# Four tables of places by kind of slot, the next head's norm at the end of short slots, and the experts' rows transposed two parts ahead

## The reference

```python
x = x + xcond(layernorm(x), cond, ctx)        # 6 layers
x = x + ffn(layernorm(x), ...)                # 8 experts, top 2 of 8, capacity 640

def xcond(x, emb, context):
    for i in range(6):
        xn = adaln(x, emb, n1_w[i], n1_b[i])
        q, k, v = split(xn @ qkv_w[i].T)                      # 16 heads of 16
        x = x + attn(rope(q), rope(k), v) @ so_w[i].T
        xn = adaln(x, emb, n2_w[i], n2_b[i])
        q, k, v = rope(xn @ cq_w[i].T), rope(context @ ck_w[i].T), context @ cv_w[i].T
        x = x + attn(q, k, v) @ co_w[i].T
        xn = adaln(x, emb, n3_w[i], n3_b[i])
        x = x + gelu(xn @ f1_w[i].T + f1_b[i]) @ f2_w[i].T + f2_b[i]

def adaln(x, emb, w, b):
    g, be = split(emb @ w.T + b)
    return ln(x) * (1 + g) + be

def ffn(x):      # router, then per expert: gelu(rows @ w1 + b1) @ w2 + b2, gated and added to the tokens' rows
```

## Time and profile before

| | |
|---|---|
| median of 3 runs | 4456.39 us |
| lowest, highest | 4449.91, 4459.43 us |
| profiled execution | 4442.28 us, span 4440.6 us |
| busy TensorE, VectorE, ScalarE, GpSimd | 89%, 65%, 58%, 19% |
| mean granted TensorE clock | 0.962 |
| layers, to the end of slot 48 | about 4070 us from the start |
| experts' rows begin to be loaded | 4242.3 us |

### The profile page before, as it was taken

How to read it: one execution, slowest core, us unless ns; L and a number is a source line. 1 busy time by engine, 2 the same in 40 slices (tenths; PEclk the granted TensorE clock), 3 DMA queues, 4 the chain that set the end, 5 groups by cost and what they waited for, 6 DMA issues and landing times. The chain is left out here.

```text
span 4440.6 us, 68492 instructions
## 1 busy us (share of the span) xinstructions
PE 3940.5 (89%) x20630; PEld 1833.7 (41%) x20630; DVE 2907.1 (65%) x4711; ACT 2561.9 (58%) x4302; POOL 857.7 (19%) x518
## 2 busy tenths in 40 slices
PE   3699999999999999999999999999999999997467
PEld 1233344533344533345433345433345433354355
DVE  3777766677766678766678766678766677752311
ACT  1376656667666567666567665567666566654122
POOL 4312121112121112211111211111211121200133
PEclk7799999999999999999999999999999999999689
DMA  5354323244323244332244332244332344410234
GB/s 162 85 135 108 97 69 78 63 108 120 87 78 72 60 113 119 87 80 65 67 108 116 94 72 66 68 108 116 97 75 59 74 129 111 109 30 13 83 99 95
DMA packets 271578, 396.39 MB, mean 89 GB/s; under 512 B 28312, under 2 KB 218400, under 8 KB 270880
## 3 DMA queue, kind: packets, MB, share of 16 engines
q1 hardware_dynamic: 263904, 382.18, 34.1%
q0 software_dynamic: 7296, 9.51, 1.3%
HBM read 226.63 MB, written 170.67 MB: 89 GB/s over the span
## 5 line engine op out<-in xcount | busy, mean ns | idle before, releaser
L837 ACT ACTIVATE prob<-ps 128x512 f32<-128x512 f32 x3072 | 1768.2, 596 | 1225.2 <-PE ps L761 1207.6
L999 DVE TENSOR_REDUCE negmax<-ps 128x2 f32<-128x1024 f32 x1536 | 1836.7, 1219 | 217.6 <-PE ps L788 195.2
L761 PE MATMUL ps<-qstack,kstack 114*128 114x512 bf16 x3072 | 1162.4, 389 | 100.1 <-ACT prob L837 84.8
L774 PE MATMUL psv<-prob,v 128*32 128x512 f32 x6144 | 829.5, 612 | 0.0
L761 PEld LDWEIGHTS ps<-qstack,kstack 114*128 114x128 bf16 x3072 | 284.6, 97 | 1190.3 <-ACT prob L837 794.5
L616 POOL TENSOR_TENSOR rot<-ropep 128x512 f32<-128x512 f32 x96 | 122.5, 1276 | 2486.7 <-DVE ropep L1032 2467.7
L788 PE MATMUL ps<-kstack,qstack 49*128 49x512 bf16 x3072 | 496.8, 388 | 97.9 <-DVE negmax L999 76.8
L736 PE MATMUL side<-anat,wf 128*128 128x256 f32 x1536 | 377.1, 388 | 9.9 <-DVE hT L1037 8.9
L1037 DVE TENSOR_SCALAR hT<-side,f1b 128x256 f32<-128x256 f32 x384 | 168.2, 479 | 303.6 <-PE side L736 303.6
L747 PE MATMUL side<-wf,hT 128*128 128x256 f32 x1536 | 347.9, 379 | 2.8 <-DVE x L1044 1.6
L736 PEld LDWEIGHTS side<-anat,wf 128*128 128x128 f32 x1536 | 285.6, 192 | 65.7 <-DVE hT L1037 30.9
(11 more groups left out here) (158 smaller groups left out, 3722.1 us busy)
## 6 DMA issues: line engine op xcount, KB each, us to landing
bounce<-parts SPq DMA_DIRECT2D x480, 256.0 KB, 2.5
qstack<-bounce SPq DMA_DIRECT2D x384, 192.0 KB, 5.5
kstack<-bounce SPq DMA_DIRECT2D x384, 192.0 KB, 6.1
bounce<-low SPq DMA_DIRECT2D x96, 256.0 KB, 2.1
ctxT<-in_ctxT SPq DMA_DIRECT2D x24, 512.0 KB, 3.9
nw<-in_nwT SPq DMA_DIRECT2D x18, 512.0 KB, 11.3
w<-in_w SPq DMA_DIRECT2D x16, 512.0 KB, 4.8
wself<-in_wself SPq DMA_DIRECT2D x24, 256.0 KB, 4.0
```

What stands on the lines that cost most here:

```text
L761: nc.tensor.matmul(ps2[:, n % RING2, :], kk[0:ROWS, h, kt * P:(kt + 1) * P], q[0:ROWS, h, :], start=True, stop=True).then_inc(s_p2full, 1)
L774: mm = nc.tensor.matmul(psv[32 * i:32 * i + 32, 0, :], v[j % 2][:, kt, (HD + 1) * h:(HD + 1) * h + 32], prob[:, 4 * (u % 2) + i, :], start ...
L837: nc.scalar.activation(prob[:, 4 * (u % 2) + i, :], ps2[:, n % RING2, :], ACT.Exp, scale=HD ** -0.5).then_inc(s_prob, 1)
L999: nc.vector.tensor_reduce(out_at, ps1[:, 2 * (n % 2):2 * (n % 2) + 2, :], AX, ALU.max, negate=True).then_inc(s_p1free, 1)
```

## The change

The two tables become four, by the kind of the slot and of the one before: `SHORT`, `SHORT_AFTER_LONG`, `LONG` and `LONG_AFTER_LONG`. Each also holds the places of the shift (M), the splits, gelu and the norms. In short slots the norm for the **next** slot's HT stands at halves 22 to 28 (`LN_NEXT`), unless the next slot follows a long one; a slot after a long one does its own at halves 0 to 5 (`LN_HT`). In long slots HT moves from 6 and 8 to 11 and 12, T2 and O move two halves earlier, LT and its norm move by one or two. In short slots HQ, HK, T2 move by up to two halves. VectorE does both reductions of a unit first when its even half has a chunk of HQ, HK, O, F1 or F2. In the experts `gather_T` and `read_T` of part n+2 stand ahead of `outputs` and `biased` of part n.

```diff
-SHORT_PLACES = {
-    "HV": [1, 3], "T1": [2, 4, 5, 7], "HT": [6, 8], "HQ": [9, 10], "HK": [12, 14],
-    "T2": [15, 17], "O": [19, 21],
+SHORT = {
+    "M": [23, 0], "HV": [1, 3], "T1": [2, 4, 6, 8], "HT": [5, 7], "HQ": [9, 11], "HK": [13, 15],
+    "T2": [16, 18], "O": [19, 21], "SPLIT": (13, 15, 19, 21),
+    "LN_NEXT": dict(stats=[22, 22, 23, 23], aggregate=24, guess=25, newton=26, tiles=[27, 27, 28, 28]),
 }
-LONG_PLACES = {
-    "HV": [1, 3], "T1": [2, 4, 5, 7], "HT": [6, 8], "T2": [9, 10], "O": [11, 12], "HQ": [13, 14],
-    "HK": [15, 16], "LT": [17, 18], "F1": [19, 20, 21, 22, 23, 24, 25, 26], "F2": [27, 28, 30, 31],
+SHORT_AFTER_LONG = {
+    "M": [24, 0], "HV": [1, 3], "T1": [2, 4, 6, 8], "HT": [7, 9], "HQ": [10, 12], "HK": [14, 16],
+    "T2": [17, 18], "O": [20, 21], "SPLIT": (14, 16, 20, 22),
+    "LN_HT": dict(stats=[0, 0, 0, 0], aggregate=1, guess=2, newton=3, tiles=[3, 4, 4, 5]),
+    "LN_NEXT": dict(stats=[22, 22, 23, 23], aggregate=24, guess=25, newton=26, tiles=[27, 27, 28, 28]),
 }
-SHORT_SHIFT, LONG_SHIFT = (23, 0), (29, 0)
-NORM_PLACES = {
-    "HT": dict(stats=[0, 0, 1, 1], aggregate=1, newton=3, tiles=[3, 3, 4, 4]),
-    "LT": dict(stats=[12, 12, 12, 12], aggregate=13, newton=15, tiles=[15, 15, 16, 16]),
+LONG = {
+    "M": [29, 0], "HV": [1, 3], "T1": [2, 4, 5, 6], "T2": [7, 8], "O": [9, 10], "HT": [11, 12], "HQ": [13, 14],
+    "HK": [15, 17], "LT": [16, 18], "F1": [19, 20, 21, 22, 23, 24, 25, 26], "F2": [27, 28, 30, 31],
+    "SPLIT": (16, 18, 20, 22), "GELU": (23, 27),
+    "LN_LT": dict(stats=[10, 10, 10, 10], aggregate=11, guess=12, newton=13, tiles=[13, 14, 14, 15]),
 }
-GUESS_PLACES = {"HT": 2, "LT": 14}
-SHORT_SPLIT = (13, 15, 18, 20)
-LONG_SPLIT = (16, 18, 20, 22)
-GELU_PLACES = (23, 27)
+LONG_AFTER_LONG = {**LONG, "LN_HT": dict(stats=[0, 0, 0, 0], aggregate=1, guess=2, newton=3, tiles=[3, 4, 4, 5])}
...
+            after_long = k < 2 or is_ffn(k - 1) or k == 2
+            return ((SHORT, SHORT_AFTER_LONG), (LONG, LONG_AFTER_LONG))[is_ffn(k)][after_long]
...
-                    if p1:
+                    both = any(what in ("HQ", "HK", "O", "F1", "F2") for what, c in plan[2 * u])
+                    if p1 and half == 0:
                         maximum(k, at)
-                        if at == 17:
-                            shift_parts(k, 0)
+                        if both:
+                            maximum(k, at + 1)
+                    if p1 and half == 1 and not both:
+                        maximum(k, at)
+                    if p1 and at == 16:
+                        shift_parts(k, 0)
...
             gather_T(0)
             hidden(0)
+            gather_T(1)
             for n in range(len(PARTS)):
                 if n + 1 < len(PARTS):
-                    gather_T(n + 1)
                     hidden(n + 1)
+                if n + 2 < len(PARTS):
+                    gather_T(n + 2)
                 outputs(n)
...
+            read_T(0)
+            read_T(1)
             gates(0)
-            read_T(0)
             for n in range(len(PARTS)):
-                if n + 1 < len(PARTS):
-                    if n % 2 == 1:
-                        gates((n + 1) // 2)
-                    read_T(n + 1)
+                if n + 2 < len(PARTS):
+                    read_T(n + 2)
+                    if n % 2 == 0:
+                        gates(n // 2 + 1)
                 biased(n)
```

More of the change, by code:

```diff
@@ L394, in is_ffn, with places_of, norm_steps @@
             return k >= 2 and is_cross(k - 2)
+        def places_of(k):
+            after_long = k < 2 or is_ffn(k - 1) or k == 2
+            return ((SHORT, SHORT_AFTER_LONG), (LONG, LONG_AFTER_LONG))[is_ffn(k)][after_long]
+        def norm_steps(k):
+            steps, places = [], places_of(k)
+            if "LN_HT" in places and k + 1 < 2 * NJ:
+                steps.append((k, "HT", places["LN_HT"]))
+            if "LN_LT" in places:
+                steps.append((k, "LT", places["LN_LT"]))
+            if "LN_NEXT" in places and "LN_HT" not in places_of(k + 1) and k + 2 < 2 * NJ:
+                steps.append((k + 1, "HT", places["LN_NEXT"]))
+            return steps
         def slot_chunks(k):
@@ L399, in slot_chunks @@
             tail, head = k >= 2, k + 1 < 2 * NJ
-            places = LONG_PLACES if is_ffn(k) else SHORT_PLACES
+            places = places_of(k)
             plan = {i: [] for i in range(2 * SLOT_UNITS)}
@@ L416, in slot_chunks @@
                 put("HT", "HQ", "HK")
-            shift_places = LONG_SHIFT if is_ffn(k) else SHORT_SHIFT
             if p2:
-                plan[shift_places[1]].append(("M", 1))
+                plan[places["M"][1]].append(("M", 1))
             if p1:
-                plan[shift_places[0]].append(("M", 0))
+                plan[places["M"][0]].append(("M", 0))
             if is_ffn(k):
@@ L917, in slot @@
                 ffn = is_ffn(k)
-                splits = LONG_SPLIT if ffn else SHORT_SPLIT
+                places = places_of(k)
+                splits = places["SPLIT"]
                 for at in range(2 * SLOT_UNITS):
@@ L930, in slot @@
                         side_work(k, what, c)
[L931 to L934, removed]
+                    for of, what, steps in norm_steps(k):
+                        if at == steps["guess"]:
+                            rstd_guess(of, what)
                     if head and at in splits:
@@ L937, in slot @@
                         (hi, mid)[step](k + 1, n)
-                    if ffn and at in GELU_PLACES:
-                        gelu(k, GELU_PLACES.index(at))
+                    if ffn and at in places["GELU"]:
+                        gelu(k, places["GELU"].index(at))
             run_slots(act, place, head0, slot)
@@ L962, in stats @@
                         wait_read(dve, place, k, "O", 1)
+                    elif "LN_HT" not in places_of(k):
+                        wait_read(dve, place, k - 1, "O", 1)
                     elif steps[0]:
@@ L1068, in slot @@
                 plan = slot_chunks(k)
-                ffn = is_ffn(k)
                 for at in range(2 * SLOT_UNITS):
                     u, half = divmod(at, 2)
-                    if p1:
+                    both = any(what in ("HQ", "HK", "O", "F1", "F2") for what, c in plan[2 * u])
+                    if p1 and half == 0:
                         maximum(k, at)
-                        if at == 17:
-                            shift_parts(k, 0)
+                        if both:
[4 more added lines that the diff above has]
+                        shift_parts(k, 0)
                     for what, c in plan[at]:
                         side_work(k, what, c)
[L1078 to L1081, removed]
+                    for of, what, norm in norm_steps(k):
                         for t in range(TT):
-                            if at == places["stats"][t]:
-                                stats(k, what, t)
-                        if at == places["aggregate"]:
+                            if at == norm["stats"][t]:
+                                stats(of, what, t)
+                        if at == norm["aggregate"]:
                             aggregate(what)
-                        if at == places["newton"]:
-                            normalise(k, what)
+                        if at == norm["newton"]:
+                            normalise(of, what)
                         for t in range(TT):
-                            if at == places["tiles"][t]:
-                                normed(k, what, t)
+                            if at == norm["tiles"][t]:
+                                normed(of, what, t)
                 if p1:
```

## The result

The changed kernel takes 4464.73 us (median of 20 runs, 4457.06 to 4469.98), the kernel before, run beside it, 4454.17 us (20 runs, 4445.0 to 4467.27). The ratio is 1.0023, with a 95% interval of 1.0015 to 1.0031: slower by 0.2%. The forecast was 4384 us.

A forecast was written before the change was run, and what follows sets the result against it. TensorE, busy 89% of the span, was taken as the bound, so only its waits cost time. Terms -20 - 29 - 7 - 4 - 12 = -72 us gave 4370 us profiled, 4384 us as median, range 4325 to 4440.

The forecast's parts named there:

- Moved past queues: SyncE's writes and loads move with `mid`; cover before the next slot's scores shrinks; priced at nothing, else 6 x 1 us.
- The other two signs that I had named: Signs of being wrong: short slots above 66.4 us, or long slots moving by over 1 us.
- Experts: Experts: transposes of part n+2 ahead of `outputs` of part n remove the copy wait from parts 2 to 15; -20 us.
- Short slots, halves 4 to 21: Short slots: waits of 4.21 us go, new ones of 1.75 come; gain 2.45 us a slot.
- Halves 22 to 31: End of short slots: the next head's norm on VectorE and its guess on ScalarE cost 0.85 us a slot.
- the six after long slots: Short slots after long ones keep a norm at the start and gain less: 1.2 us each, -7 us.
- Long slots: Long slots: `normed` leaves GpSimd's residual but new waits come; 0.2 us a slot, -4 us, plus -12 from fewer clock dips.
- The sum: Whole kernel: all terms together -72 us on the profiled execution, 4442.3 to 4370; as median 4384 us.
- (e): Rival: the clock falls more often, every long slot taking 99.0 us; 4427 us, chance 0.09.
- (d): Rival: VectorE becomes the bound at its new places, the norm ending short slots showing fully; +56, 4512 us, chance 0.08.
- (a): Rival: the new waits in the layers do not come; 4336 us, chance 0.16.
- The port rule: VectorE and GpSimd share ports; the first to start blocks the other; third tile of long slots held up to 1.26 us.

The follow-up runs named there:

- the run that mends it alone: Changed kernel with the load of M's rows ahead of the next head's ten loads in SyncE's queue, in short slots: 4407.78 us, ratio 0.9899.
- the run at half 19: Changed kernel with the first shift of M in short slots at half 19 instead of 16: 4393.86 us, ratio 0.9863.
- the repaired kernel: Changed kernel with the first shift of short slots at half 19 and M's rows ahead of the next head's loads: 4322.9 us, ratio 0.9691.

## Why the prediction was wrong

**The step that failed** is "Moved past queues", with what it left out. I wrote of SyncE's queue "I price it at nothing; if this cover is gone it costs 6 x 1 us", after looking at when the next head's loads land. They did land in time. What stands behind them in the queue is M's rows, and I had not followed it. It cost 16 waits and 38.6 us in brackets behind slot 1, and 57 us by the run that mends it alone. And the move of the shift from half 17 to 16 is in the diff and in no step of mine: I had counted its three operations at 0.6 us at the end of a slot and priced their first copy, in the middle, nowhere, though the row of before that shows it at 1.06 us was there to be read. The move alone is worth 71 us by the run at half 19. Without these two faults the same change takes 4322.9 us, so together they are worth 142 us. The other two signs that I had named came as well: short slots over 66.4 us, and slot 6 shorter by 3.2.

**The clock** is the second half of both. Short slots went from 13.7 to 135.8 us at the lower clock, and back to 27.3 with the repairs, or 69.0 and 92.2 with one of them. I had taken stalls of 2.76 us in long slots as its cause and had asked only whether those shrink; I had not asked where the change makes new ones of that length. It makes one of 2.2 to 2.5 us in every short slot. That the lower clock goes with these stalls is seen in time (the one of slot 4 ends at 427.04, the lower clock is there from 427.3 on) and in its going away with them. It does not follow each: 17 of the 24 stalls have it beside them, 7 do not, slot 5 among them. No run changed the clock alone.

**Point by point.** *Experts*, -20: measured -22.0 and -23.5; a pair of parts takes 18.3 us (4315.13 to 4333.47, two starts of `hidden`), the forecast was 18.7, and the waits left are 1.3 us in parts 0 and 1. *Short slots, halves 4 to 21* (slot 4 of the repaired kernel): the new waits that I had worked out are there, at half 6 and 8 0.22, at 14 0.47, at 16 0.48 us, and at 18 a smaller one; up to the end of half 21 the slot is 2.6 us shorter, the forecast was 2.45. *Halves 22 to 31*: 0.75 at half 26 for the reduction, 0.51 there for the exponential and 0.50 at half 30; the stretch takes 15.9 us for 15.2, the forecast was 16.1. A short slot of the repaired kernel is 64.46 us, the forecast 64.8; its 24 short slots together give -34.5, the forecast -36, though the six after long slots give nothing (+1.6 for -7) and the others more. *Long slots*, -4 and -12 for the clock: -49. HQ's second chunk (half 14), HK's first (15) and LT (16 and 18) in slot 7:

```profile
650.12 1.99 PE L684 MATMUL side<-xnT,wself 128*128 128x512 f32 x4 [0.40 <-DVE ropep L1049]
654.49 1.98 PE L684 MATMUL side<-xnT,wself 128*128 128x512 f32 x4 [0.85 <-DVE ropep L1049]
659.00 0.65 PE L678 MATMUL side<-ident,hT 128*128 128x128 f32 x4 [1.45 <-DVE hT L1006]
664.29 0.66 PE L678 MATMUL side<-ident,hT 128*128 128x128 f32 x4 [0.30 <-DVE ropep L1049]
```

HK's first chunk waits 1.02 us from start to start against the forecast 1.1, and LT at 18 0.47 against 0.5: these two are right. LT at 16 waits 1.6 against 2.1 (2.76 before), and of the 0.45 that I had put on halves 4 to 8 and 12 only 0.1 came. So a long slot after a long one gains 1.0 us and not 0.2; one after a short slot gains 1.9, since its norm now stands in the slot before, for which I had credited nothing. That makes 15 x 1.0 + 6 x 1.9 = 26 of the 49. The other 23 are the clock: I took 12 back of 21, and all 54.6 us at the lower level went. These are figures of one execution each: with the layers unchanged, the long slots of the run with the experts alone have 81.9 us at the lower level, so the clock's part of the gain is known roughly only. *The sum* would have been -72; with the two faults mended it is -118. So the rest of the forecast was not right either, 46 us too small, by the long slots (32 more), the start of the layers (12, which comes with asking for M's rows first: 231.9 us to slot 2 with that repair alone) and the experts (3).

Of the rivals, (e) had the right engine and the wrong place: the clock fell more often, in short slots and not in long ones. (d) had the right side only. VectorE was late at a new place, but for the shift and not for the norm. The repaired kernel is nearest to (a) in number (4322.9 against 4336) and not in cause: the new waits that (a) leaves out are there.

The port rule that I had used for one tile holds for the shift too, and I had not applied it there. The rows show a cast of 1.18 and of 2.14 us that ends 0.04 us after GpSimd's operation, and a subtraction of 1.20 us that ends 0.04 after the next. The Trainium skill, SBUF — State Buffer, section "Who interferes with whom", names casts among what can take the shared pair, and `tensor_tensor` with both inputs in SBUF among what contends with GpSimd's reads; the trace agrees, down to 32 elements a partition.

## What to carry to other kernels

List every instruction whose place the diff changes, the small ones too, and for each what stands behind it on its engine or queue: the loads that moved were in time, and the request behind them was not. An operation that a neighbour may hold for 2 us costs nothing where nothing behind it is soon wanted, as at half 17, and is dear ahead of anything that TensorE waits for: here the second reduction of a unit in one kind of slot, and the read of a side chunk in the other. Where TensorE is the bound and at its upper clock, a stall of 2 to 3 us that a change makes in each repetition has to be priced twice, for itself and for the clock beside it, which fell at 17 of 24 such stalls here.

## What was not expected of the hardware

Two operations on 128x32 elements take 0.17 and 0.19 us by themselves and, in the rows above, 1.1 to 2.1 us when they begin while GpSimd is at an elementwise operation on SBUF: they end 0.04 to 0.05 us after it. Reductions from PSUM beside such an operation are not lengthened (in the kernel before, 2.35 us for two from 418.47 on, beside L617 of GpSimd from 418.48 to 419.75; 1.22 us for one otherwise). And small loads are not quick behind large ones: M's rows, 8 KB a request, took 5.1 to 6.8 us from their second issue to the last update in the trace behind ten loads for the stacks, and 1.9 us ahead of them.
